# An FP4 fake-quantization moved wholly to VectorE, and its software pipelining taken out, in an attention + FFN block on eight cores

## The chip, the cores and the metric

The kernel runs on eight cores of one Trainium2 chip (two dies of four cores). Every core runs the same program on two of the sixteen sequences; nothing is exchanged between cores. The metric is the device time in microseconds of the slowest core. A core has TensorE (PE, matmuls and transposes), VectorE (DVE), ScalarE (ACT), GpSimd (POOL, here a little arithmetic in one stage and the issue of stores) and SyncE (SP, the issue of loads), each with its own in-order instruction stream. The streams meet only in semaphores.

## The reference

Input x is 16 x 2048 x 1024 in f32. Both branches start from the same LayerNorm, and their sum goes onto x:

```python
xn = _layernorm(x)
x = x + attn(xn, Wqkv, bqkv, Wproj, bproj, mapping) + ffn(xn, w_gate, w_up, w_down)

def fp4_quant_dequant(x):          # blocks of 16 along the last dim
    xb = x.reshape(shape[:-1] + (shape[-1] // 16, 16))
    scale = jnp.maximum(jnp.max(jnp.abs(xb), axis=-1, keepdims=True) / 6.0, 1e-12)
    xn = xb / scale
    idx = jnp.searchsorted(_MID, jnp.abs(xn))     # _MID  = .25 .75 1.25 1.75 2.5 3.5 5
    return (_GRID[idx] * jnp.sign(xn) * scale).reshape(shape)   # _GRID = 0 .5 1 1.5 2 3 4 6
def fp4_linear(x, w):
    return einsum('bsk,nk->bsn', fp4_quant_dequant(x), fp4_quant_dequant(w))
def ffn(x):
    h = silu(fp4_linear(x, w_gate)) * fp4_linear(x, w_up)      # 1024 -> 2816
    return fp4_linear(h, w_down)                               # 2816 -> 1024
```

The attention gathers queries and 64 keys per block of 64 rows by a Hilbert mapping, 16 heads of 64.

## The kernel before

A core has 4096 rows, 32 tiles of 128. After a short setup the stages follow each other with barriers between them:

- **Stage A** (once for each of the two sequences, 16 tiles each). A tile of x is loaded by SyncE. VectorE takes statistics (L448 to L455), ScalarE the square root (L484), VectorE applies them (L457, into `sc2`) and casts to bf16 (L462). The normalized tile is transposed on TensorE (L543) and multiplied with Wqkv in six chunks of 512 columns (L530, L533), each evacuated by ScalarE (L504) before POOL stores the tile to `qkv_dram`. The same tile is also quantized, transposed (L551), evacuated (L493, L517) and stored to `xqT_dram` for the FFN. Both transposes use the one PSUM tile `psT`.
- **Stages B and C** (once a sequence): gathers and attention, output projection, residual; the sum goes to `partial_dram`.
- **Weight stage**: 68 pieces of w_gate, w_up and w_down are quantized and transposed into SBUF. Here POOL adds up the three sign tiles.
- **Stage D** (32 tiles). SyncE loads the quantized transposed tile and the partial sum of tile gt. The load waits for the store of tile gt-2 (by the semaphore `sp`). TensorE computes three pairs of gate and up chunks (two chunks of 512, in the third pair 512 and 256; L1128), ScalarE takes Silu of the gate chunks (L1194, L1195) into `pairbuf`, and VectorE multiplies them with the up chunks (L1251, L1253) and quantizes the product into `hq2`. The quantized product of tile gt-1 is transposed in three groups (L1149), evacuated (L1208), multiplied with w_down (L1164), and added to the partial sum by VectorE (L1270, L1271), after which POOL stores it.

**Quantization.** Seven thresholds decide the level of a squared scaled value: four (`TL`) count 1 each, three (`TSQ`) count 1, 1 and 2 doubled. It is split in three helpers. `_q_pre` (VectorE, 5 instructions) takes the block maxima, scale and reciprocal, and the scaled value `v`. `_q_scal` (ScalarE, 4) squares `v` and takes Sign of the square against the three `TSQ` thresholds. A fifth ScalarE instruction takes the sign of `v`. `_q_post` (VectorE, 9 in stages A and D) adds up the `TL` compares in `sc5`, adds the three sign tiles, multiplies by the sign and by half the scale.

**Pipelining.** In A and D the quantization of a tile spreads over two rounds. VectorE's stream in round t is statistics, apply, `_q_pre` of tile t, then `_q_post` of tile t-1 (in D the same by pairs). ScalarE's stream in round t of stage A is: root of t; sign of t-1; evacuation of the quantized transpose of t-2; evacuation of the normalized transpose of t-1; six evacuations of QKV of t-1; `_q_scal` of t. TensorE's is: QKV of t-1; transpose of the normalized tile t; transpose of the quantized tile t, which waits for `_q_post` of t. In D ScalarE has for each pair: sign of the pair before; two Silus; `_q_scal` (its Sign tiles have one buffer and wait for the last `_q_post`); evacuation of one transpose group. TensorE has pairs 0 and 1 of gt, three transpose groups of gt-1, pair 2 of gt, the down product of gt-1. The values that semaphores have to reach are counted ahead in tables (`EVA`, `EVD`).

Of the kernel before, what the change touches and what calls it, by code (L numbers as in the profile page):

```python
# [8 lines left out]
F32 = mybir.dt.float32  # L9
BF16 = mybir.dt.bfloat16  # L10
# [12 lines left out]
NKC = D // 128  # L23
# [8 lines left out]
QPOST_S = 9  # L32
# [85 lines left out]
def build_nc(stage=9):  # L118
# [25 lines left out]
    with ExitStack() as st:  # L144
# [22 lines left out]
        uneg = sb("uneg", [128, 16], F32)  # L167

# [171 lines left out]
        with ExitStack() as g1:  # L340
# [40 lines left out]
            for seq in range(NSEQ if stage >= 5 else (1 if (stage >= 2 or stage >= 30) else 0)):  # L381
                if True:
# [4 lines left out]
                    vAb = [sc3, vA2]  # L387
                    a2Ab = [sc4, sc6]
# [3 lines left out]
                    svA, ssA, stnA, ldA, lgA, spA, sqA = sv.v, ss.v, stn.v, ld.v, lg.v, sp.v, sq.v  # L392

                    EVA = {}
                    cs, cv, cp, cq = ssA, svA, stnA, sqA
                    for t in range(T + 1):
                        if t <= T - 1:
                            cv += 5; EVA[("recip", t)] = cv
                            cv += 1; EVA[("apply", t)] = cv
                            cv += 1; EVA[("xnbf", t)] = cv  # L400
                            cv += QPRE_INCS; EVA[("v", t)] = cv
                        if t >= 1:
                            cv += QPOST_S
                            EVA[("post", t - 1)] = cv
                            EVA[("L3", t - 1)] = cv - 5
                            EVA[("srel", t - 1)] = cv - 2
                            EVA[("q1", t - 1)] = cv - 1
                        if t <= T - 1:
                            cs += 1; EVA[("rstd", t)] = cs
                        if t >= 1:  # L410
                            cs += 1; EVA[("sgn", t - 1)] = cs
                        if t >= 2:
                            cs += 1; EVA[("xqTev", t - 2)] = cs
                        if t >= 1:
                            cs += 1; EVA[("xnTev", t - 1)] = cs
                            for oc in range(6):
                                cs += 1; EVA[("qkvev", t - 1, oc)] = cs
                        if t <= T - 1:
                            cs += 1; EVA[("a2", t)] = cs
                            cs += 3; EVA[("s3", t)] = cs  # L420
                        if t == T:
                            cs += 1; EVA[("xqTev", T - 1)] = cs
                        if t >= 1:
                            for oc in range(6):
                                cp += 1; EVA[("qkvchunk", t - 1, oc)] = cp
                        if t <= T - 1:
                            cp += 1; EVA[("txn", t)] = cp
                            cp += 1; EVA[("txq", t)] = cp
                    ldav = lambda t: ldA + 16 * (t + 1)

                    with nc.Block() as blk:
                        @blk.sync
                        def _(sync):
                            for t in range(T):
                                if t >= 1:
                                    sync.wait_ge(ld.h, ldav(t - 1))
                                if t >= 2:
                                    sync.wait_ge(sv.h, EVA[("apply", t - 2)])
# [5 lines left out]
                        def _(vec):  # L444
                            for t in range(T + 1):
                                if t <= T - 1:
                                    vec.wait_ge(ld.h, ldav(t))
                                    sv.inc(vec.bn_stats(stats[:, 0:6], xbA[t % 2][:, 0:512]))  # L448
                                    sv.inc(vec.bn_stats(stats[:, 6:12], xbA[t % 2][:, 512:1024]))
                                    vec.wait_ge(sv.h, sv.v)  # L450
                                    sv.inc(vec.bn_aggr(stats[:, 12:14], stats[:, 0:12]))
                                    vec.wait_ge(sv.h, sv.v)
                                    sv.inc(vec.tensor_scalar_add(stats[:, 14:15], stats[:, 13:14], 1e-5))
                                    vec.wait_ge(sv.h, sv.v)
                                    sv.inc(vec.reciprocal(stats[:, 15:16], stats[:, 14:15]))  # L455
# [872 lines left out]
```

## Time and profile before

| | us |
|---|---|
| median of 3 runs | 6145.74 |
| lowest, highest | 6119.06, 6185.59 |
| the profiled execution | 6171.19 |
| span of its slowest core (core 7) | 6169.6 |
| span of its fastest core (core 0) | 6036.1 |

The profile is that of core 7. The busy time of an engine counts its instructions, not its waits. Lists of instructions in order of time give start, duration, engine, line, operation, output and inputs, and in brackets how long the engine stood idle before it and whose end released it. A time between two starts on one engine is a duration with its gap.

### The profile page before, as it was taken

Reading aid. Unit: us, or ns where it says so; the run is one execution under the profiler, and the core shown is the slowest. Engines: PE = TensorE matmul, PEld = TensorE weight load, DVE = VectorE, ACT = ScalarE, POOL = GpSimd, SP = SyncE. Lnnn points to the kernel's source line nnn. Section 1 sums busy time; section 2 is a strip of 40 time slices with the busy share of each in tenths; the row PEclk is TensorE's granted clock in tenths of the full one; section 3 lists DMA queues with packets and bytes.
Section 4 is the critical chain, followed back from the end, with each engine's and each line's share of the span. In section 5 each row is a group of like instructions: output and inputs, shape, how many; then the busy total and the mean of one; then the engine's idle time right before and its main releaser. Section 6 shows DMA issues by size and latency. Waiting matters only on the chain. (4 is left out here: it accounts for less than half of the span.)

```text
span 6169.6 us, 39885 instructions; the slowest of 8 cores (6036.1 to 6169.6 us)
## 1 busy us (share of the span) xinstructions
PE 2254.8 (37%) x12373; PEld 1094.2 (18%) x12373; DVE 3222.5 (52%) x3408; ACT 1567.2 (25%) x2218; POOL 713.2 (12%) x453
## 2 busy tenths in 40 slices
PE   1444447444444400000004444344344344344344
PEld 0111243111134100000001111112112112112111
DVE  2444332444423599999996544543544544544544
ACT  1222221222222133333432222221221221221221
POOL 0000011000011244444440000000000000000000
PEclk9666656666655755555556666666667667667666
DMA  4111113111111401101100000000000000000000
GB/s 75 37 41 39 43 47 111 55 40 41 39 51 42 133 27 31 31 28 29 32 25 13 15 17 17 9 17 17 9 17 17 9 17 17 9 17 17 9 17 16
DMA packets 86057, 196.70 MB, mean 32 GB/s; under 512 B 42295, under 2 KB 42311, under 8 KB 85847
## 3 DMA queue, kind: packets, MB, share of 16 engines
q1 hardware_dynamic: 59304, 93.42, 5.6%
q0 software_dynamic: 26544, 100.74, 5.2%
q8 instruction: 102, 1.67, 0.1%
q14 instruction: 107, 0.88, 0.0%
HBM read 135.41 MB, written 67.12 MB: 33 GB/s over the span
## 5 line engine op out<-in xcount | busy, mean ns | idle before, releaser
L98 DVE SCALAR_TENSOR_TENSOR sc<-sc 128x1024 f32<-128x1024 f32 (+1 forms) x588 | 691.8, 1176 | 62.7 <-DVE sc L98 1.4
L1251 DVE TENSOR_TENSOR sc<-pairbuf,psU 128x512 f32<-128x512 f32 x96 | 66.1, 688 | 1000.8 <-ACT pairbuf L1194 1000.8
L1164 PE MATMUL psA<-wdqT,hqT 128*128 128x512 bf16 x1408 | 386.4, 445 | 497.1 <-ACT hqT L1208 496.0
L969 PE MATMUL psT<-ident,wq_bf 128*128 128x128 bf16 x528 | 67.1, 306 | 1118.1 <-DVE wq_bf L115 1118.1
L1194 ACT ACTIVATE pairbuf<-psQ 128x512 f32<-128x512 f32 x96 | 56.8, 592 | 1213.6 <-PE psB L1128 1213.6
L1149 PE MATMUL psT<-ident,hq 128*128 128x128 bf16 x704 | 77.0, 273 | 781.6 <-ACT hqT L1208 771.4
L1279 POOL DMA_DIRECT2D out<-sc x32 | 17.1, 533 | 2897.2 <-DVE sc L1271 2805.4
L457 DVE TENSOR_SCALAR sc<-sc,stats 128x1024 f32<-128x1024 f32 x32 | 26.0, 813 | 562.4 <-ACT stats L484 562.4
L1164 PEld LDWEIGHTS psA<-wdqT,hqT 128*128 128x128 bf16 x1408 | 154.0, 111 | 722.7 <-issue 607.9
L969 PEld LDWEIGHTS psT<-ident,wq_bf 128*128 128x128 bf16 x528 | 50.9, 137 | 1134.3 <-issue 1134.3
L72 ACT ACTIVATE s1D<-sc,qbias 128x1024 bf16<-128x1024 f32 (+1 forms) x96 | 103.7, 1080 | 564.3 <-DVE sc L107 564.2
L530 PE MATMUL psQ<-Wqkv_sb,xnT 128*128 128x512 bf16 x768 | 239.2, 468 | 0.0
L504 ACT CAST qkv_tile<-psQ 128x512 bf16<-128x512 f32 x96 | 56.4, 587 | 674.0 <-PE psQ L533 674.0
L1270 DVE TENSOR_TENSOR sc<-psA,sc 128x512 f32<-128x512 f32 x32 | 22.1, 692 | 380.2 <-PE psA L1164 380.2
L1128 PE MATMUL psQ<-wgqT,attn_tm 128*128 128x512 bf16 x384 | 146.7, 551 | 198.7 <-DMA sc<-partial_dram 170.3
L80 POOL TENSOR_TENSOR sc<-s1W,s2W 128x1024 f32<-128x1024 bf16 (+1 forms) x68 | 147.2, 2164 | 620.3 <-DVE sc L98 451.5
L1128 PE MATMUL psQ<-wgqT,sexp 128*128 128x512 bf16 x384 | 145.0, 545 | 194.3 <-DMA sc<-partial_dram 174.9
L68 ACT ACTIVATE sc<-sc 128x1024 f32<-128x1024 f32 x132 | 134.7, 1020 | 293.7 <-DVE sc L63 293.6
L551 PE MATMUL psT<-ident,xq_tm 128*128 128x128 bf16 x256 | 32.4, 306 | 463.6 <-DVE xq_tm L115 463.6
L1149 PEld LDWEIGHTS psT<-ident,hq 128*128 128x128 bf16 x704 | 59.4, 122 | 801.3 <-issue 793.8
L530 PE MATMUL psU<-Wqkv_sb,xnT 128*128 128x512 bf16 x768 | 198.6, 405 | 0.0
L115 DVE TENSOR_TENSOR wq_bf<-sc,bstats 128x1024 bf16<-128x1024 f32 (+1 forms) x68 | 191.1, 2810 | 7.5 <-DVE sc L113 0.5
(192 smaller groups left out, 6258.4 us busy)
## 6 DMA issues: line engine op xcount, KB each, us to landing
sc<-xin SPq DMA_DIRECT2D x64, 512.0 KB
qkv_dram<-qkv_tile POOLq DMA_DIRECT2D x32, 768.0 KB, 4.5
partial_dram<-sc POOLq DMA_DIRECT2D x32, 512.0 KB, 3.8
sc<-partial_dram SPq DMA_DIRECT2D x32, 512.0 KB
out<-sc POOLq DMA_DIRECT2D x32, 512.0 KB, 3.0
wrow<-wg SPq DMA_DIRECT2D x22, 512.0 KB
wrow<-wu SPq DMA_DIRECT2D x22, 512.0 KB
xqT_dram<-xqTst POOLq DMA_DIRECT2D x32, 256.0 KB, 4.9
```

The costliest lines, as they stand in the source:

```text
L68: ss.inc(scal.activation(a2_ap, v_ap, AF.Square))
L72: ss.inc(scal.activation(s1_ap, a2_ap, AF.Sign, bias=qbias[:, 0:1]))
L80: sq.inc(g.tensor_tensor(u[:, 0:n], s1[:, 0:n], s2[:, 0:n], ALU.add))
L98: sv.inc(vec.scalar_tensor_tensor(L[:, 0:n], a2[:, 0:n], c, L[:, 0:n], ALU.is_gt, ALU.add))
L115: sv.inc(vec.tensor_tensor(seg(out_bf), seg(L[:, 0:n]), bc(hsc), ALU.mult))
L530: tensor.matmul(pq[:], xnTA[(t - 1) % 2][:, 128 * c:128 * (c + 1)], Wqkv_sb[:, c, 512 * oc:512 * (oc + 1)], start=(c == 0), stop=False)
L969: m = tensor.transpose(psT[:, 128 * k:128 * (k + 1)], wqW[c % 2][:, 128 * k:128 * (k + 1)], ident[:])
L1128: m = tensor.matmul(dst, xqb[gt % 2][:, 128 * c:128 * (c + 1)], w_src[:, c, i0:i0 + iw], start=(c == 0), stop=(c == NKC - 1))
L1149: m = tensor.transpose(psT[:, 128 * c:128 * (c + 1)], hq2[:, (gt - 1) % 2, 128 * (8 * g + c):128 * (8 * g + c + 1)], ident[:])
L1164: m = tensor.matmul(psA[:, 512 * oc:512 * (oc + 1)], hqT[:, 128 * c:128 * (c + 1)], wdqT[:, c, 512 * oc:512 * (oc + 1)], start=(c == 0), s ...
L1194: ss.inc(scal.activation(pb2[:, 0:iwA], gbank[0][:, 0:iwA], AF.Silu))
L1251: sv.inc(vec.tensor_mul(sc2[:, 0:iwA], pb2[:, 0:iwA], psU[:, 0:iwA]))
```

## The change

The pipelining of the quantization in stages A and D is taken out, and a single function of 19 VectorE instructions does all of it. Of these, `tensor_reduce` and three small ones prepare the scales, and 15 go over the whole tile.

```diff
+def _emit_quant(vec, x_ap, nblk, bstats, v, a2, L, S, out_bf, sv):
...
+    sv.inc(vec.tensor_reduce(sc, seg(x_ap), AX.X, ALU.max, apply_absolute_value=True))
+    vec.wait_ge(sv.h, sv.v)
+    sv.inc(vec.tensor_scalar(sc, sc, 1.0 / 6.0, 1e-12, ALU.mult, ALU.max))
+    vec.wait_ge(sv.h, sv.v)
+    sv.inc(vec.reciprocal(rsc, sc))
+    sv.inc(vec.tensor_scalar_mul(hsc, sc, 0.5))
+    vec.wait_ge(sv.h, sv.v)
+    sv.inc(vec.tensor_tensor(seg(v[:, 0:n]), seg(x_ap), bc(rsc), ALU.mult))
+    vec.wait_ge(sv.h, sv.v)
+    sv.inc(vec.tensor_mul(a2[:, 0:n], v[:, 0:n], v[:, 0:n]))
+    vec.wait_ge(sv.h, sv.v)
+    sv.inc(vec.tensor_single_scalar(L[:, 0:n], a2[:, 0:n], TL[0], ALU.is_gt))
+    for c in TL[1:]:
+        vec.wait_ge(sv.h, sv.v)
+        sv.inc(vec.scalar_tensor_tensor(L[:, 0:n], a2[:, 0:n], c, L[:, 0:n], ALU.is_gt, ALU.add))
+    sv.inc(vec.tensor_single_scalar(S[:, 0:n], a2[:, 0:n], TSQ[2], ALU.is_gt))
+    for c in (TSQ[1], TSQ[0], TSQ[2]):
+        vec.wait_ge(sv.h, sv.v)
+        sv.inc(vec.scalar_tensor_tensor(S[:, 0:n], a2[:, 0:n], c, S[:, 0:n], ALU.is_gt, ALU.add))
+    vec.wait_ge(sv.h, sv.v)
+    sv.inc(vec.scalar_tensor_tensor(L[:, 0:n], S[:, 0:n], 2.0, L[:, 0:n], ALU.mult, ALU.add))
+    sv.inc(vec.tensor_single_scalar(a2[:, 0:n], v[:, 0:n], 0.0, ALU.is_gt))
+    vec.wait_ge(sv.h, sv.v)
+    sv.inc(vec.tensor_scalar(a2[:, 0:n], a2[:, 0:n], 2.0, -1.0, ALU.mult, ALU.add))
+    vec.wait_ge(sv.h, sv.v)
+    sv.inc(vec.tensor_mul(L[:, 0:n], L[:, 0:n], a2[:, 0:n]))
+    vec.wait_ge(sv.h, sv.v)
+    sv.inc(vec.tensor_tensor(seg(out_bf), seg(L[:, 0:n]), bc(hsc), ALU.mult))
```

Stage A: VectorE quantizes tile t right after the cast of tile t, and there is no post in the next round. ScalarE loses the four activations of `_q_scal` and the sign; the evacuation of the quantized transpose of t-1 comes at the end of round t, after the six of QKV.

```diff
 @blk.scalar
 def _(scal):
     for t in range(T + 1):
         if t <= T - 1:
-            scal.wait_ge(sv.h, EVA[("recip", t)])
+            scal.wait_ge(sv.h, cva(t) + 5)
             ss.inc(scal.activation(stats[:, 14:15], stats[:, 15:16], AF.Sqrt))
         if t >= 1:
-            if t >= 2:
-                scal.wait_ge(sv.h, EVA[("q1", t - 2)])
-            ss.inc(scal.activation(sgnA[:], vAb[(t - 1) % 2][:], AF.Sign))
...
-        if t <= T - 1:
-            scal.wait_ge(sv.h, EVA[("v", t)])
...
-            _q_scal(scal, vAb[t % 2][:], a2Ab[t % 2][:],
...
+            scal.wait_ge(stn.h, txqv(t - 1))
+            ss.inc(scal.copy(xqTA[(t - 1) % 2][:], psT[:]))
```

Stage D: VectorE quantizes each pair's product in one go. ScalarE loses its five activations a pair and takes two copies more: it brings the up chunks from PSUM into a `pairbuf` twice as wide, and VectorE's product reads both factors from there. TensorE has the pairs 0, 1, 2 of gt, then the transposes and the down product of gt-1. ScalarE evacuates the three transpose groups after the three pairs.

```diff
+                ss.inc(scal.activation(pb2[:, 0:iwA], gbA[:, 0:iwA], AF.Silu))
+                ss.inc(scal.activation(pb2[:, 512:512 + iwB], gbB[:, 0:iwB], AF.Silu))
+                ss.inc(scal.copy(pb2[:, 1024:1024 + iwA], psU[:, 0:iwA]))
+                ss.inc(scal.copy(pb2[:, 1536:1536 + iwB], psB[:, 512:512 + iwB]))
...
-                sv.inc(vec.tensor_mul(sc2[:, 0:iwA], pb2[:, 0:iwA], psU[:, 0:iwA]))
+                vec.wait_ge(ss.h, spair(gt, pq, 2))
+                sv.inc(vec.tensor_mul(sc2[:, 0:iwA], pb2[:, 0:iwA], pb2[:, 1024:1024 + iwA]))
+                vec.wait_ge(ss.h, spair(gt, pq, 3))
...
+                _emit_quant(vec, sc2[:, 0:pw], pw // 16, bstats,
+                            sc3, sc4, sc5, sc6,
+                            hq2[:, gt % 2, pair_cols[pq][0]:pair_cols[pq][0] + pw], sv)
```

In both stages a load still waits for what it waited for, in D for the store of tile gt-2. In the weight stage only the offsets inside `bstats` change (72 to 88, 144 to 176, 288 to 352). The second buffers of `v` and the sign tiles of A and D are gone, and `maskU` is allocated earlier.

## Rows read from the trace of the kernel before

**Rows 1.** The page's busy times: us, share of the span, instructions.

```profile
PE 2254.8 (37%) x12373; PEld 1094.2 (18%) x12373; DVE 3222.5 (52%) x3408; ACT 1567.2 (25%) x2218; POOL 713.2 (12%) x453
```

**Rows 2.** Stretches: length, busy us (count) by engine, granted clock, DMA share, GB/s.

```profile
98.75:705.72 606.97, 263.46 (x1058) 103.83 (x1058) 271.58 (x336) 167.49 (x218) 21.66 (x30) 0.68 0.12 39
1102.25:1703.15 600.90, 256.85 (x1058) 102.89 (x1058) 271.58 (x336) 167.50 (x218) 21.67 (x30) 0.66 0.12 40
3257.56:6162.56 2905.00, 1231.62 (x5190) 552.05 (x5190) 1381.69 (x1600) 645.47 (x775) 16.54 (x31) 0.69 0.05 15
```

**Rows 3.** In order of time, stage A, VectorE: start, us, line, idle before.

```profile
475.02 1.23 DVE L115 TENSOR_TENSOR xq_tm<-sc,bstats 128x1024 bf16<-128x1024 f32 x1
476.16 0.69 DVE L448 BATCH_NORM_STATS2 stats<-sc 128x6 f32<-128x512 f32 x1
...
497.94 0.81 DVE L457 TENSOR_SCALAR sc<-sc,stats 128x1024 f32<-128x1024 f32 x1 [19.65 <-ACT stats L484]
...
499.65 1.22 DVE L56 TENSOR_REDUCE bstats<-sc 128x64 f32<-128x1024 f32 x1
```

**Rows 4.** The same stretch, TensorE and ScalarE.

```profile
462.45 1.01 ACT L497 COPY xnT<-psT 128x1024 bf16<-128x1024 bf16 x1 [1.25 <-PE psT L543]
...
476.54 1.01 PE L551 MATMUL psT<-ident,xq_tm 128*128 128x128 bf16 x8 [14.17 <-DVE xq_tm L115]
...
477.34 3.38 PE L530 MATMUL psQ<-Wqkv_sb,xnT 128*128 128x512 bf16 x8
...
480.97 1.90 PE L530 MATMUL psU<-Wqkv_sb,xnT 128*128 128x512 bf16 x8
...
492.82 0.59 ACT L504 CAST qkv_tile<-psU 128x512 bf16<-128x512 f32 x1 [1.98 <-PE psU L533]
...
497.64 0.19 ACT L484 ACTIVATE stats<-stats 128x1 f32<-128x1 f32 x1
```

**Rows 5.** The instructions of line L1270: min/median/max ns, first and last start.

```profile
L1270 DVE TENSOR_TENSOR sc<-psA,sc x32: 691/692/693, 3389.4 to 6161.3; 128x512 f32<-128x512 f32 x32
```

**Rows 6.** Who waited for whom: us in total, times, longest.

```profile
DVE sc L1251 <- ACT pairbuf L1194: 1000.8, 96, 20.8
```

**Rows 7.** In order of time, stage D, VectorE and TensorE.

```profile
3513.96 0.69 DVE L1251 TENSOR_TENSOR sc<-pairbuf,psU 128x512 f32<-128x512 f32 x1 [2.51 <-ACT pairbuf L1194]
...
3515.34 1.22 DVE L56 TENSOR_REDUCE bstats<-sc 128x64 f32<-128x1024 f32 x1
...
3517.68 1.23 DVE L63 TENSOR_TENSOR sc<-sc,bstats 128x1024 f32<-128x1024 f32 x1
3519.01 0.69 DVE L95 TENSOR_SCALAR sc<-sc 128x1024 f32<-128x1024 f32 x1
...
3519.81 3.88 DVE L98 SCALAR_TENSOR_TENSOR sc<-sc 128x1024 f32<-128x1024 f32 x3
...
3539.48 0.69 DVE L1251 TENSOR_TENSOR sc<-pairbuf,psU 128x512 f32<-128x512 f32 x1 [9.08 <-ACT pairbuf L1194]
...
3540.61 0.95 DVE L56 TENSOR_REDUCE bstats<-sc 128x48 f32<-128x768 f32 x1
...
3542.55 0.96 DVE L63 TENSOR_TENSOR vD<-sc,bstats 128x768 f32<-128x768 f32 x1
...
3576.29 3.53 PE L1128 MATMUL psQ<-wgqT,sexp 128*128 128x512 bf16 x8 [9.80 <-DMA sc<-partial_dram]
...
3585.85 0.69 DVE L1251 TENSOR_TENSOR sc<-pairbuf,psU 128x512 f32<-128x512 f32 x1 [17.90 <-ACT pairbuf L1194]
...
6136.60 0.69 DVE L1270 TENSOR_TENSOR sc<-psA,sc 128x512 f32<-128x512 f32 x1 [11.93 <-PE psA L1164]
```

**Rows 8.** VectorE by line and form, busy us, mean ns: weight stage, setup.

```profile
L101 DVE SCALAR_TENSOR_TENSOR sc<-sc 128x1024 f32<-128x1024 f32 x60 | 180.3, 3006 | 6.2
...
L262 DVE TENSOR_SCALAR map_rowf<-map_rowf 1x2048 f32<-1x2048 f32 x1 | 1.2, 1214 | 0.1
```

**Rows 9.** The page's DMA issues: count, KB each, us to landing.

```profile
xqT_dram<-xqTst POOLq DMA_DIRECT2D x32, 256.0 KB, 4.9
```

More of the change, by code:

```diff
@@ new lines, in build_nc, with cva, csa, cpa @@
+                    svA, ssA, stnA, ldA, lgA, spA = sv.v, ss.v, stn.v, ld.v, lg.v, sp.v
+                    def cva(t):
+                        return svA + 26 * t
+                    def csa(t):
+                        return ssA + (9 * t - 8 if t >= 1 else 0)
+                    def cpa(t):
+                        return stnA + (8 * t - 6 if t >= 1 else 0)
+                    def sc_off(t):
+                        return 1 if t <= T - 1 else 0
+                    rstdv = lambda t: csa(t) + 1
@@ L429, in build_nc @@
+                    xnTev = lambda tm1: csa(tm1 + 1) + sc_off(tm1 + 1) + 1
+                    qkvev = lambda tm1, oc: csa(tm1 + 1) + sc_off(tm1 + 1) + 2 + oc
+                    xqTev = lambda tm1: csa(tm1 + 1) + sc_off(tm1 + 1) + 8
+                    qkvchunk = lambda tm1, oc: cpa(tm1 + 1) + oc + 1
+                    txnv = lambda t: cpa(t) + (6 if t >= 1 else 0) + 1
+                    txqv = lambda t: txnv(t) + 1
                     ldav = lambda t: ldA + 16 * (t + 1)
@@ new lines, in build_nc, with cpf, csf, cvf @@
+            svD, ssD, stnD, ldD, soutD, spD = sv.v, ss.v, stn.v, ld.v, sout.v, sp.v
+            def cpf(gt):
+                v = stnD
+                for g in range(gt):
+                    v += (3 if g <= NTOT - 1 else 0) + (4 if g >= 1 else 0)
+                return v
+            def csf(gt):
+                v = ssD
+                for g in range(gt):
+                    v += (12 if g <= NTOT - 1 else 0) + (3 if g >= 1 else 0)
+                return v
+            def cvf(gt):
+                v = svD
+                for g in range(gt):
+                    v += (63 if g <= NTOT - 1 else 0) + (2 if g >= 1 else 0)
+                return v
@@ new lines, in pairv, with tgroup, down_done, spair @@
+            def pairv(gt, pq):
+                return cpf(gt) + pq + 1
+            def tgroup(gtm1, g):
+                gt = gtm1 + 1
+                return cpf(gt) + (3 if gt <= NTOT - 1 else 0) + g + 1
+            def down_done(gtm1):
+                return tgroup(gtm1, 2) + 1
+            def spair(gt, pq, k):
+                return csf(gt) + 4 * pq + k + 1
+            def evacv(gtm1, g):
+                gt = gtm1 + 1
+                return csf(gt) + (12 if gt <= NTOT - 1 else 0) + g + 1
@@ L1083, in ldv, with hmultv, quantdonev, addsv @@
+            def hmultv(gt, ci):
+                pq, k = ci // 2, ci % 2
+                return cvf(gt) + 21 * pq + k + 1
+            def quantdonev(gt):
+                return cvf(gt) + 63
+            def addsv(gtm1):
+                return cvf(gtm1 + 1) + 63 * (1 if gtm1 + 1 <= NTOT - 1 else 0) + 2
             def ldv(gt):
@@ L1204, in _ @@
[L1204 to L1217 removed]
+                                    gbA = gbank[0]
```

430 lines of the change are left out of this document (113 added, 317 removed).

## The prediction

> **What bounds the kernel now.** I read the page's busy times first [rows 1]: VectorE leads with 3222.5 us of 6169.6, only 52%, so no engine is full, and the question is in which stage VectorE is full and in which it waits. The stretches by stage [rows 2] answer that. The two passes of stage A (LayerNorm, quantize, QKV) take 607.0 and 600.9 us with VectorE busy 271.6 in each, 45%; stage D (the FFN) takes 2905.0 us with VectorE busy 1381.7, 48%. TensorE is at 43% in all three. So in A and D the time is set by a loop of waits. The rest (setup, attention, projection, weight quantization; 2057 us by difference) is the same in both kernels but for offsets of buffers. I take it as unchanged.
>
> Stage A's VectorE rows show the loop [rows 3]: a tile takes 607.0 / 16 = 37.9 us there, of which 19.65 are one wait for ScalarE's square root L484 (at 497.94). ScalarE's and TensorE's rows [rows 4] show why: the root of tile t+1 stands behind the four activations of `_q_scal`, these behind the six evacuations of QKV of tile t-1, and these behind the matmuls, which need `_q_post` of t-1 for the transpose ahead of them. VectorE does that post in the same round. Everything is in one ring.
>
> Stage D's adds stand at 3389.4 (first) and 6161.3 (last) [rows 5]. The last tile has no tile behind it, and its adds come 24.7 us after those before (6136.60 [rows 7]), so a tile takes (6161.3 - 24.7 - 3389.4) / 30 = 91.6 us. VectorE's waits inside it: L1251 1000.8 us in 96 waits [rows 6], 31.3 a tile. 2.5 of them come ahead of the second pair, 9.1 ahead of the third, and about 19.7 ahead of the first. The last is seen in [rows 7]: after the adds store and load run, TensorE starts 3576.29, L1251 3585.85, 17.90 us after the adds' end; the longest is 20.8 [rows 6].
>
> **The change, part by part.** It does three things: (a) quantization goes wholly to VectorE (`_emit_quant`, 19 instructions for 14, the compares against `TSQ`, the square and the sign among them); (b) each tile is quantized in one go, not half in the next round, so ScalarE has only the root and evacuations in A, and Silu and evacuations in D; (c) in D ScalarE also copies the up product out of PSUM, and TensorE's third pair moves ahead of the transposes.
>
> Cost of one quantization of 1024 columns, start to start, from [rows 7]. Reduce to scaled value is 3515.34 to 3517.68, 2.34, with the three small ones inside. A two-input operation behind a wait takes 1.33 (3517.68 to 3519.01), a one-input compare 0.80 (3519.01 to 3519.81). The new function has 11 of the first kind (scaled value, square, 3+3 compare-adds, combine, sign multiply, output) and 4 of the second. Two kinds are new. A compare without a second constant is in setup, 2048 f32 elements in 1.21 us (L262 [rows 8]), 0.59 ns each, the rate of the 0.69 row, so it keeps that price. A tile multiplied by itself has no row: 1.23 as any two-input operation, or, as it reads one tile, 0.69 at the least; I take 1.23, for it is still a two-input instruction, and keep 0.54 x 128 = 68 us for the range's low side. Three instructions wait for nothing just before them (the first `S` compare, the sign compare, the next tile's first); such a one starts about 0.09 before the former's end instead of 0.10 after (475.02 + 1.23 against 476.16 [rows 3]), 0.19 less each. 2.34 + 11 x 1.33 + 4 x 0.80 - 0.57 = 19.6 us. For 768 columns: 1.94 (3540.61 to 3542.55) + 11 x 1.06 + 4 x 0.66 (estimated from 0.80 by the ratio of the long ones) - 0.57 = 15.7.
>
> Stage A, VectorE alone: statistics 497.94 - 19.65 - 476.16 = 2.13, the root's round trip 0.4 (0.30 from L484's start to L457's [rows 3, 4], and a hop before), apply and cast 1.71 (497.94 to 499.65), quantization 19.6: 23.8 us a tile. Is anything slower? The root of t+1 starts a second chain: evacuation of xnT 1.01, transpose and QKV up to the last evacuation 476.54 to 492.82, 16.3, its 0.6, the evacuation of xqT (of the size of xnT's) 1.0, hops 0.2, about 19.1, after which ScalarE is free for root t+2. That is 4.7 under 23.8. SyncE's load waits for the apply of t-2, a round early. POOL's two stores stand behind the xqT evacuation at 19.1, take 1.4 to issue (21.66 / 30 each [rows 2]) and 4.9 to land [rows 9]: 1.6 into the next round, where the first QKV evacuation, which waits for them, is due at 1.2 + 4.4 (476.54 to 480.97, where the second chunk follows [rows 4]) = 5.6. So 4.0 spare. A pass is 16 x 23.84 and about 1 for its start, an estimate, 382.5, against 607.0 and 600.9: minus 224.5 and minus 218.4, together 443. Ends are alike: after the last quantization transpose, QKV and stores follow in both.
>
> Stage D, VectorE alone: from the product to the reduce 1.38 (1024) and 1.13 (768) [rows 7], so 2 x 21.0 + 16.8 + adds 1.3 = 60.1 us. The two waits inside a tile (2.5, 9.1) and the one before the adds go: TensorE has 38.5 us of work a tile (1231.6 / 32 [rows 2]), with this tile's pairs first and then the transposes and the down product of the one before, while VectorE quantizes for 59. The wait ahead of the first pair stays, because the load of gt+1 waits for the store of gt-1, that for the adds of gt-1, and VectorE does these after quantizing gt. It grows: the product now waits for Silu A, Silu B and the copy of the up half instead of Silu A. ScalarE starts 0.49 apart and a copy of this size out of PSUM is about 0.59, so 0.97 (bounds: 0.5, one start apart, and 1.2, two whole ones). 20.0 (between 19.7 and 20.8) + 1.0 + 60.1 = 81.1 against 91.6, 30 times: minus 315. The ends I take as cancelling: the first two tiles, which wait for no store, lose a few us by the longer quantization, and the last, whose product needs no post after the adds before it, gains as many.
>
> Sum: 6169.6 - 443 - 315 = 5412 us of span. The profiled execution ran 1.6 over its span, 6171.2, and that is 25.5 over the median of the runs, 6145.7. That gives 5388, and I say 5390, for the median.
>
> What is hidden costs if its cover goes: were it the TensorE chain in A that ends last, each us beyond 4.7 costs 32; each us that the first pair is late costs 30.
>
> **Rivals.**
> TensorE slows. Its first eight matmuls behind a gap take 3.38 at 1.2 GHz, the later eights 1.9 at 2.4 GHz [rows 4]; the granted clock of both stages is 0.66 to 0.69 [rows 2]. In D its gap before the first pair grows from 9.8 [rows 7] to some 35 us. Against: it falls back after the present gaps already, and comes up within the first eight or ten. If it never came up, A's chain would be 19.1 + 5 x 1.7 = 27.6, 3.8 over, times 32 = 120; D's first pair 3 x 1.7 = 5 later, times 30 = 150: 5660.
>
> POOL and VectorE hinder each other. In the weight stage, where POOL computes, one combine takes 3.01 us [rows 8] against 1.23. In A POOL issues 1.4 us of stores a tile into a VectorE that now has no gap. If VectorE stood still for them: 46 us; if they landed twice as late (9.8), 0.9 beyond the spare, 29 us more: 5465. Against: the stores already issue beside VectorE's work at unchanged durations. The Trainium skill, SBUF — State Buffer, section "SBUF: two separate sides", says that a DMA issued by GpSimd cannot write its descriptors while VectorE runs an operation in a two-port mode, and gives 620 ns that became some 3100. The kernel adds three such one-input operations to each quantization. By that page's figures a store would be 2.5 us late, an estimate, and be inside the spare. No row here shows such a wait; the 4.9 us are what the stores take now.
>
> The other side: the tiles stay chained. Should the root still come only after the newest QKV, A keeps its 19.65 us: 23.4 + 19.7 = 43.1 against 37.8, plus 5.3 x 32 = 170; should D keep its 2.5 and 9.1, it is 92.7 against 91.6, plus 33: 6350. VectorE's added work then shows bare (4.5 us per 1024, some 550 in all). It decides from 758 us of waits that stay, 11.8 a tile over the 64 of both stages. For it speaks only that the ring exists now; against it, that no instruction on ScalarE ahead of the root needs VectorE's output of the same round any more.
>
> **How the numbers follow.** My forecast 80%, TensorE slow 7%, POOL 7%, chained 4%, something unseen 2%. The forecast's own range: the wait before the first pair 17.9 to 20.8 (minus 63, plus 24), the copy (minus 15, plus 6), a gap of 0.10 off by 0.02 in 16 places of 128 quantizations (41 either way); not all at their ends at once, 5300 to 5440. The square at 0.69 (minus 68) would reach the low end with any other of these. The POOL case and the first part of the TensorE case are taken in: 5300 to 5520. About 1% is what a measurement of this kernel tells from no change. Faster 0.95, same 0.01, slower 0.04.
>
> **What would show it.** In the new trace: no wait of VectorE for the root beyond 0.4; an A pass of 383 us with VectorE at 97%; quantizations of 19.6 us; in D one wait of 19 to 22 us a tile and nearly none else, period 81; VectorE busy near 3770, ScalarE far below its 1567 (five activations a quantization go, two copies a pair come in D), POOL unchanged. I am wrong if A's round is set by the evacuation of xqT, if QKV's evacuation waits for stores, or if the first pair of a tile takes over 11 us.

## The result and the profile after

| | us |
|---|---|
| after, median of 10 runs | 5374.68 (5364.07 to 5386.49) |
| before, median of 10 runs | 6117.34 (6068.37 to 6185.59) |
| ratio, 95% interval | 0.8797 [0.8769, 0.8825] |
| profiled execution after: span of its slowest core (core 3) | 5362.1 |

The forecast was 5390, 15 us above. The profiled spans differ by 6169.6 - 5362.1 = 807.5 us, where the working had 758. The 6169.6 belongs to one of the longer executions of before, in which cores 4 to 7 ran for a median of 6155.7 and cores 0 to 3 for 6042.4 with the same program (after: 5354.2 and 5355.0).

The page's busy times, after (columns as in [rows 1]):

```profile
PE 2114.4 (39%) x12373; PEld 1039.0 (19%) x12373; DVE 3737.3 (70%) x4048; ACT 1030.1 (19%) x1770; POOL 716.4 (13%) x453
```

The stretches of the first pass of stage A and of stage D, after (columns as in [rows 2]):

```profile
96.95:480.36 383.41, 244.94 (x1058) 96.71 (x1058) 341.20 (x416) 85.50 (x138) 21.68 (x30) 0.81 0.19 61
2835.00:5355.00 2520.00, 1119.80 (x5147) 506.40 (x5145) 1760.37 (x2079) 268.82 (x476) 16.55 (x31) 0.72 0.05 16
```

VectorE has 515 us more to do than in [rows 1], and the kernel is 743 us faster in the medians. Both stages have given up waits. VectorE's waits after (us in total, times, longest), where [rows 6] had 1000.8 in 96:

```profile
DVE sc L1154 <- ACT pairbuf L1133: 598.3, 31, 21.0
DVE sc L1166 <- PE psA L1109: 17.2, 1, 17.2
DVE sc L471 <- ACT stats L488: 15.8, 32, 1.7
```

Before's waits for the root were 562.4 us in 32 (one of them the 19.65 us of [rows 3]); they have shrunk to 15.8. In stage D one wait a tile is left.

**Stage A.** A pass is 383.4 us (first statistics 96.95, those of the second pass 480.36), against the 607.0 and 600.9 of [rows 2]. ScalarE in one tile, in order of time, beside VectorE's first statistics and its apply:

```profile
312.91 0.69 DVE L462 BATCH_NORM_STATS2 stats<-sc 128x6 f32<-128x512 f32 x1
315.12 0.20 ACT L488 ACTIVATE stats<-stats 128x1 f32<-128x1 f32 x1 [5.26 <-DVE stats L469]
315.43 0.81 DVE L471 TENSOR_SCALAR sc<-sc,stats 128x1024 f32<-128x1024 f32 x1 [0.40 <-ACT stats L488]
...
332.17 0.59 ACT L497 CAST qkv_tile<-psU 128x512 bf16<-128x512 f32 x1 [1.27 <-PE psU L516]
332.65 1.02 ACT L500 COPY xqTst<-psT 128x1024 bf16<-128x1024 bf16 x1
339.28 0.20 ACT L488 ACTIVATE stats<-stats 128x1 f32<-128x1 f32 x1 [5.61 <-DVE stats L469]
```

A VectorE tile is 336.71 - 312.91 = 23.80 us. The chain of the other engines, from the root to the end of the evacuation of the quantized transpose, is 315.12 to 333.67 = 18.55 us, and after it ScalarE stands idle for 5.61 us until the next root can start. In [rows 3] and [rows 4] it was VectorE that stood and the root that was late.

**Stage D.** One handover between tiles, all engines in order of time (SPq is SyncE's queue):

```profile
4141.64 0.68 DVE L1167 TENSOR_TENSOR sc<-psA,sc 128x512 f32<-128x512 f32 x1
4142.88 0.53 POOL L1174 DMA_DIRECT2D out<-sc  x1 [79.96 <-DVE sc L1167]
4146.00 0.37 SPq L1054 DMA_DIRECT2D attn_tm<-xqT_dram  x1
4150.48 3.57 PE L1083 MATMUL psQ<-wgqT,attn_tm 128*128 128x512 bf16 x8 [38.93 <-DMA sc<-partial_dram]
4159.65 0.60 ACT L1131 ACTIVATE pairbuf<-psQ 128x512 f32<-128x512 f32 x1 [59.30 <-PE psB L1083]
4160.62 0.59 ACT L1133 COPY pairbuf<-psU 128x512 f32<-128x512 f32 x1
4161.31 0.69 DVE L1154 TENSOR_TENSOR sc<-pairbuf 128x512 f32<-128x512 f32 x1 [19.00 <-ACT pairbuf L1133]
4180.44 1.86 PE L1109 MATMUL psA<-wdqT,hqT 128*128 128x512 bf16 x4 [1.23 <-ACT hqT L1139]
```

The 19.00 us of VectorE's idle time have parts that can be read here: 3.7 us from the end of the adds until SyncE issues the load, for which the store has to be issued and to land (4142.3 to 4146.0), 4.5 until TensorE, waiting for that load, starts (4150.48), 9.2 for the first pair (4159.65), 1.7 for the two Silus and the copy. The down product begins at 4180.44 and ends about 12 us later; the next adds come at 4220.09. So the wait inside a tile and the wait ahead of the adds [rows 7] are gone. The adds of the tiles run from 2951.6 to 5335.44 (the last but one): 30 periods of 79.5 us, where it was 91.6.

### The profile page after: what moved, and what is told of

Same layout as the page of the kernel before. It is cut to its first block and busy times, and to the rows that moved or that the text cites. A ratio compares the mean times of both kernels' runs of the same rounds, so it can differ in the third digit from the quotient of the medians.

```text
span 5362.1 us, 39202 instructions; the slowest of 8 cores (5347.6 to 5362.1 us)
## 1 busy us (share of the span) xinstructions
PE 2114.4 (39%) x12373; PEld 1039.0 (19%) x12373; DVE 3737.3 (70%) x4048; ACT 1030.1 (19%) x1770; POOL 716.4 (13%) x453
## 5 line engine op out<-in xcount | busy, mean ns | idle before, releaser
L1154 DVE TENSOR_TENSOR sc<-pairbuf 128x512 f32<-128x512 f32 x96 | 66.0, 688 | 598.3 <-ACT pairbuf L1133 598.3
L73 DVE SCALAR_TENSOR_TENSOR sc<-sc 128x1024 f32<-128x1024 f32 (+1 forms) x384 | 444.8, 1158 | 41.1 <-DVE sc L70 0.9
L69 DVE SCALAR_TENSOR_TENSOR sc<-sc 128x1024 f32<-128x1024 f32 (+1 forms) x384 | 444.8, 1158 | 41.1 <-DVE sc L69 1.4
L1131 ACT ACTIVATE pairbuf<-psQ 128x512 f32<-128x512 f32 x96 | 57.3, 597 | 2139.1 <-PE psB L1083 1927.3
L1083 PE MATMUL psQ<-wgqT,sexp 128*128 128x512 bf16 x384 | 117.1, 460 | 609.6 <-DMA sc<-partial_dram 579.8
L1083 PE MATMUL psQ<-wgqT,attn_tm 128*128 128x512 bf16 x384 | 116.5, 458 | 609.2 <-DMA sc<-partial_dram 566.5
L135 DVE SCALAR_TENSOR_TENSOR sc<-sc 128x1024 f32<-128x1024 f32 (+1 forms) x204 | 247.0, 1211 | 22.3 <-DVE sc L135 0.9
L150 DVE TENSOR_TENSOR sc<-sc,sgnW 128x1024 f32<-128x1024 f32 (+1 forms) x68 | 184.3, 2711 | 14.4 <-DVE sc L138 10.9
L121 POOL TENSOR_TENSOR sc<-sc,s3W 128x1024 f32<-128x1024 f32 (+1 forms) x68 | 191.8, 2821 | 9.7
L119 POOL TENSOR_TENSOR sc<-sc,s3W 128x1024 f32<-128x1024 f32 (+1 forms) x68 | 190.2, 2798 | 11.2 <-POOL sc L117 2.2
L513 PE MATMUL psU<-Wqkv_sb,xnT 128*128 128x512 bf16 x768 | 187.1, 387 | 0.0
L138 DVE SCALAR_TENSOR_TENSOR sc<-sc 128x1024 f32<-128x1024 f32 (+1 forms) x68 | 182.0, 2676 | 7.1
L725 DVE TENSOR_TENSOR sc<-psA,maskU 128x1024 f32<-128x1024 f32 x16 | 19.6, 1225 | 238.0 <-PE psA L662 238.0
L1083 PEld LDWEIGHTS psQ<-wgqT,sexp 128*128 128x128 bf16 x384 | 39.3, 111 | 681.7 <-issue 659.4
```

The costliest lines, as they stand in the source:

```text
L69: sv.inc(vec.scalar_tensor_tensor(L[:, 0:n], a2[:, 0:n], c, L[:, 0:n], ALU.is_gt, ALU.add))
L73: sv.inc(vec.scalar_tensor_tensor(S[:, 0:n], a2[:, 0:n], c, S[:, 0:n], ALU.is_gt, ALU.add))
L119: sq.inc(g.tensor_tensor(u[:, 0:n], u[:, 0:n], s3[:, 0:n], ALU.add))
L121: sq.inc(g.tensor_tensor(u[:, 0:n], u[:, 0:n], s3[:, 0:n], ALU.add))
L135: sv.inc(vec.scalar_tensor_tensor(L[:, 0:n], a2[:, 0:n], c, L[:, 0:n], ALU.is_gt, ALU.add))
L138: sv.inc(vec.scalar_tensor_tensor(L[:, 0:n], u[:, 0:n], 0.0, L[:, 0:n], ALU.add, ALU.add))
```

## The experiments

All are compared with the kernel before on the same chip: its median was 6065.5 us beside e1 to e4, 6068.1 beside e0 and e5 to e7, and 6125.5 beside e8 and e9, which ran on another chip. There the seven runs of before lie between 6065 and 6177, so the ratios of e8 and e9 are less sharp than the others (see their intervals), and these two are best compared with each other. Differences in us are differences of medians.

### The two stages by themselves

e1 takes the change in stage A alone, e2 in stage D alone. Below, `-` is the call in before; the one stage takes the `+`, the other keeps the `-`.

```diff
-    _q_pre(vec, sc2[:], 64, bstats, 72 * (t % 2), vAb[t % 2], sv)        # e1: stage A
-    _q_scal(scal, vAb[t % 2][:], a2Ab[t % 2][:], ...)
-    _q_post(vec, 64, bstats, 72 * (b % 2), a2Ab[b % 2], ...)
+    _emit_quant(vec, sc2[:], 64, bstats, sc3, sc4, sc5, sc6, ...)
...
-    _q_scal(scal, vDb[Pg % 2][:, 0:pw], a2Db[Pg % 2][:, 0:pw], ...)      # e2: stage D
+    ss.inc(scal.copy(pb2[:, 1024:1024 + iwA], psU[:, 0:iwA]))
+    ss.inc(scal.copy(pb2[:, 1536:1536 + iwB], psB[:, 512:512 + iwB]))
+    _emit_quant(vec, sc2[:, 0:pw], pw // 16, bstats, sc3, sc4, sc5, sc6, ...)
```

> Only stage A is changed (quantization in one go on VectorE); stage D is as before. Theory (the change breaks a ring of waits in A and another in D, and the two gains add): a pass of A takes 383 us, D keeps its 88.5 to 92 us a tile; 5700 us, 414 less than the 6117 of before, the rest of the 742 being D's. Rival (the gain in D alone matters, or the two stages hinder each other): less than 300 us gained.

> Only stage D is changed; stage A is as before. Theory: passes of A stay at 590 to 607 us, D falls to 79.5 us a tile; 5790 us, some 328 less than before, so that this gain and that of the run with A alone add up to the 742 of the whole change within 20. Rival (they overlap): the two together are over 30 off.

> The changed kernel unedited, to stand beside its variants on one chip. 5375 us; on a chip where the kernel before takes 6065 the gain is 690 and equals the sum of the runs with A alone (421) and D alone (262) within 20.

Measured: e1 5650.69 us, ratio 0.9306 [0.9291, 0.9322]; e2 5800.46, 0.9568 [0.9552, 0.9584]; e0 5377.58, 0.8856 [0.8832, 0.888].

In medians e1 is 415 us under its before, e2 265, and the whole change 690.5. The parts add up to 680 (683, if each is worked out from its ratio), which the intervals can't tell from 690: no meddling of the two stages is seen. Stage A came out as priced (415 for 414). Stage D came out 63 us short of the 328 expected. The reason is in the profile of before itself. The price rests on its core 7. These are VectorE's waits on core 0 in the same execution:

```profile
DVE sc L1251 <- ACT pairbuf L1194: 920.3, 96, 18.3
DVE sc L457 <- ACT stats L484: 531.6, 32, 19.0
```

Core 7 has 1000.8 [rows 6] where core 0 has 920.3, 2.5 us a tile more, and its longest wait is 20.8 against 18.3. A tile of before takes 91.6 us on core 7 and 88.7 on core 0 (first adds 3341.4, last but one 6003.4), so what is worth 91.6 - 79.5 = 12.1 us a tile on core 7 is worth 9.2 on core 0: 30 x 9.2 = 276, near the 265. In e1, whose stage D is that of before, core 6 also has tiles of 88.8 us.

The wait ahead of a tile's first product is where core 7 differs: 20.6 us in all but the first five of its thirty handovers, 17.7 to 18.3 on core 0. In the mean of thirty, TensorE starts 6.0 us after the issue of the load on core 7 and 4.6 on core 0, and the first pair takes 9.6 and 8.85 us. Why, stays open.

### Was it VectorE's new work, or the order?

e3 leaves everything of before as it is but TensorE's order in stage A: QKV of tile t follows its own transpose, ahead of the quantized transpose of t. ScalarE keeps square and signs.

```diff
 @blk.tensor
 def _(tensor):
-    for t in range(T + 1):
-        if t >= 1:
-            tensor.wait_ge(ss.h, EVA[("xnTev", t - 1)])
-            for oc in range(6):                    # QKV of t-1
...
+    for t in range(T):
         ...                                        # transpose of the normalized tile t
+        tensor.wait_ge(ss.h, EVA[("xnTev", t)])
+        for oc in range(6):                        # QKV of t
...
         tensor.wait_ge(sv.h, EVA[("post", t)])     # transpose of the quantized tile t
```

> The kernel before with one edit: in stage A TensorE's QKV matmuls of a tile come ahead of the transpose of its quantized form, not behind it. ScalarE keeps its square and signs, VectorE its 11 long operations, and the quantization stays spread over two rounds. Theory (the ring of before ran through that order; where the arithmetic is done does not matter for it): the wait for the root falls from 17 us to about 5, a tile of A from 37 to 24 to 25.5 us, 5700 us. Rival (the gain in A needs the four activations to leave ScalarE, ahead of the root): at least 12 us of the wait stay, over 6000 us.

Measured: 5626.78 us, ratio 0.9283 [0.9268, 0.9299], minus 439. The stretch of a pass of stage A in e3 (columns as above):

```profile
97.10:478.50 381.40, 249.46 (x1072) 97.12 (x1073) 268.88 (x334) 167.77 (x219) 21.65 (x30) 0.80 0.20 62
```

VectorE's wait for the root in e3 (in total, times, longest):

```profile
DVE sc L456 <- ACT stats L483: 147.1, 32, 5.5
```

One root in e3 with what stands ahead of it on ScalarE and waits for it on VectorE, in order of time:

```profile
324.72 1.13 ACT L76 ACTIVATE s3A<-sc,qbias 128x1024 bf16<-128x1024 f32 x1
325.76 0.19 ACT L483 ACTIVATE stats<-stats 128x1 f32<-128x1 f32 x1
326.06 0.81 DVE L456 TENSOR_SCALAR sc<-sc,stats 128x1024 f32<-128x1024 f32 x1 [5.08 <-ACT stats L483]
```

Without moving one instruction to VectorE, stage A is as fast as in the changed kernel: a pass takes 381.4 us where that of after takes 383.4. VectorE is busy for 268.9 us of it and not for 341, and 4.6 us a tile are still spent waiting for a root that stands behind the last Sign (324.72) on ScalarE. So what stage A gained, it gained from the ring being cut. The 4.5 us of work a tile that went to VectorE took up what was left of the wait, and no more. (The same has not been tried in stage D: no run changes TensorE's order there and leaves the quantization as it was.)

### The wait that is left in stage D

e4 is the changed kernel with the two loads of a tile parted. The activations of tile gt+1 are loaded as soon as their buffer is free, and only the partial sum still waits for the store of tile gt-1. e7 does the same to the kernel before.

```diff
+def load_x(gt):
+    if gt >= 1:
+        sync.wait_ge(ld.h, ldv(gt - 1))
+    if gt >= 2:
+        sync.wait_ge(stn.h, pairv(gt - 2, 2))
+    sync.dma_start(out=xqb[gt % 2], in_=xqT_dram[...]).then_inc(ld.h, 16)
+load_x(0)
 for gt in range(NTOT):
-    if gt >= 2:
-        sync.wait_ge(sp.h, spD + gt - 1)
-        sync.wait_ge(stn.h, pairv(gt - 2, 2))
-    sync.dma_start(out=xqb[gt % 2], in_=xqT_dram[...]).then_inc(ld.h, 16)
-    sync.dma_start(out=pp[gt % 2], in_=partial_dram[...]).then_inc(ld.h, 16)
+    if gt + 1 < NTOT:
+        load_x(gt + 1)
+    if gt >= 1:
+        sync.wait_ge(lp.h, lgv(gt - 1))
+    if gt >= 2:
+        sync.wait_ge(sp.h, spD + gt - 1)
+    sync.dma_start(out=pp[gt % 2], in_=partial_dram[...]).then_inc(lp.h, 16)
```

> The changed kernel, in D with the load of the quantized tile apart from that of the partial sum: TensorE's input of tile gt+1 is loaded a tile earlier and no longer waits for the store of gt-1. Theory (the 19.2 us ahead of a tile's first product are the store, the load and the first pair in a row): all of it is hidden, a tile of D takes 60.1 us, 30 x 19.2 = 576 less: 4800 us, VectorE busy over 95% in D. Rival (another wait takes its place: TensorE has 38 us of work a tile and its first pair comes only behind the down product): 8 to 10 of the 19 stay, 5050 to 5100 us.

> The kernel before with the load of D's quantized tile apart from that of the partial sum, as in the variant of the changed kernel. Theory (in the kernel before the 18 us ahead of the first pair are store, load and first pair behind the down product; the split takes out store and load, 8.4, and TensorE's order keeps the pair of about 9 behind the down product): the wait falls from 18 to 9, minus 270, 5800 us. Rival (the store is the whole wait): minus 530. Rival (the other waits grow as much): no change.

Measured: e4 4777.0 us, ratio 0.7883 [0.7868, 0.7899], 600.6 us under e0 on the same chip. e7 5717.39, ratio 0.9409 [0.9362, 0.9457], minus 351. The handover in e4:

```profile
3549.86 0.68 DVE L1182 TENSOR_TENSOR sc<-psA,sc 128x512 f32<-128x512 f32 x1
3550.46 0.68 DVE L1169 TENSOR_TENSOR sc<-pairbuf 128x512 f32<-128x512 f32 x1
3551.11 0.53 POOL L1189 DMA_DIRECT2D out<-sc  x1 [59.45 <-DVE sc L1182]
3554.20 0.33 SPq L1072 DMA_DIRECT2D sc<-partial_dram  x1
3554.68 0.36 SPq L1059 DMA_DIRECT2D sexp<-xqT_dram  x1
```

The first product (L1169) follows the adds without a gap: its pair was done before the store was even issued. The whole 19 us were the road from the adds through store, load and pair: the adds now come every 60.1 us, as expected, where they came every 79.5. ("VectorE busy over 95% in D" was missed in the same way as the 97% of the prediction: it is 1648.08 of 1803.00 us, 91%, since the gaps between its instructions don't count.) The same handover in e7, where before's order is kept:

```profile
4059.67 5.34 PE L1179 MATMUL psA<-wdqT,hqT 128*128 128x512 bf16 x24
4064.85 1.89 PE L1143 MATMUL psQ<-wgqT,attn_tm 128*128 128x512 bf16 x8
4065.19 0.69 DVE L1285 TENSOR_TENSOR sc<-psA,sc 128x512 f32<-128x512 f32 x1 [11.99 <-PE psA L1179]
4072.77 0.69 DVE L1266 TENSOR_TENSOR sc<-pairbuf,psU 128x512 f32<-128x512 f32 x1 [6.29 <-ACT pairbuf L1209]
```

Here the load is off the path too, but TensorE has the down product of gt-1 ahead of the first pair of gt, and the adds wait for the one and the product for the other. The wait fell from 17.90 [rows 7] to 6.29, 11.6 us; times 30 that is 348, near the 351 measured, and between the 270 and the 530 of the two expectations. The theory let 9 us stay, the whole first pair behind a gap. (On core 2 of e7 all but one of the thirty waits are 6.29.) Two things make it 6.3: the first eight matmuls take 1.89 right behind the down product, where they took 3.53 behind a gap of 9.80 [rows 7], and the pair begins 0.3 us ahead of the adds (4064.85, 4065.19) and so runs beside them. What e4 has over e7 in stage D goes with the order of the changed kernel, in which the down product runs while VectorE is busy with the next tile. That it is the order alone is argued from these rows and not shown: the two kernels also differ in where the quantization is done.

### Whose time is the changed kernel's?

e5 takes the second count out of the new function, five of its 19 instructions (so its quantization knows fewer levels). e6 lets the product read the up half from PSUM, without ScalarE's two copies.

```diff
-    sv.inc(vec.tensor_single_scalar(S[:, 0:n], a2[:, 0:n], TSQ[2], ALU.is_gt))                # e5
-    for c in (TSQ[1], TSQ[0], TSQ[2]):
...
-        sv.inc(vec.scalar_tensor_tensor(S[:, 0:n], a2[:, 0:n], c, S[:, 0:n], ALU.is_gt, ALU.add))
...
-    sv.inc(vec.scalar_tensor_tensor(L[:, 0:n], S[:, 0:n], 2.0, L[:, 0:n], ALU.mult, ALU.add))
...
-    ss.inc(scal.copy(pb2[:, 1024:1024 + iwA], psU[:, 0:iwA]))                                 # e6
-    ss.inc(scal.copy(pb2[:, 1536:1536 + iwB], psB[:, 512:512 + iwB]))
...
-    sv.inc(vec.tensor_mul(sc2[:, 0:iwA], pb2[:, 0:iwA], pb2[:, 1024:1024 + iwA]))
+    sv.inc(vec.tensor_mul(sc2[:, 0:iwA], pb2[:, 0:iwA], psU[:, 0:iwA]))
```

> The changed kernel without the second count: the first S compare, its three compare-adds and the combine are left out of each quantization (the levels above 2 come out wrong), 14 instructions a quantization instead of 19, 5.9 us less on 1024 columns and 4.7 on 768. Theory (VectorE sets the end everywhere in A and D, with TensorE's and ScalarE's chain about 19 us a tile behind it in A): D falls by its full 2 x 5.9 + 4.7 = 16.5 us a tile, A only from 23.8 to 19, not to 17.9: minus 530 and minus 150, 4690 us. Rival (A has no second chain so near): 17.9 us a tile, 4655 us. Rival (VectorE is not what sets the end in D): D falls by less than half.

> The changed kernel, in D with VectorE's product reading the up chunks from PSUM as before; ScalarE's two copies a pair go, and TensorE's next up chunks wait for the product. Theory: the wait ahead of a tile's first product falls by the two instructions between Silu A and copy A, 0.97 us, and TensorE's later up chunks stay hidden: 30 x 0.97 = 29 less than the changed kernel, 5345 us. Rival (TensorE's third pair, now held until the second product 21 us later, pushes transposes and down product past the adds): slower than the changed kernel.

Measured: e5 4715.9 us, ratio 0.7774 [0.776, 0.7788], 662 under e0. e6 5335.05, 0.8795 [0.8779, 0.881], 42.5 under e0. VectorE's waits in e5, for the pair and for the root:

```profile
DVE sc L1149 <- ACT pairbuf L1128: 609.3, 31, 21.5
DVE sc L466 <- ACT stats L483: 43.3, 32, 2.5
```

And in e6, for the pair:

```profile
DVE sc L1155 <- ACT pairbuf L1133: 578.7, 31, 20.5
```

e5: a quantization of 1024 columns is 5.72 us shorter there and one of 768 is 4.53. In stage D all of it comes off the end, since the wait stays where it was, at 19.6 us ((609.3 - 21.5) / 30; 19.2 in after, 20.1 in e0): 2 x 5.72 + 4.53 = 15.97, times 31 that is 495. In stage A the wait for the root grows from 0.5 to 1.35, because the other engines' chain of 18.55 us is now longer than VectorE's work in a tile (23.80 - 5.72 = 18.1): (5.72 - 0.86) x 32 = 156. Together 651 of the 662. So in the changed kernel VectorE's own work stands bare in both stages, and in stage A about 5 us deep.

e6: its wait is 18.6 us a tile ((578.7 - 20.5) / 30), that of after 19.2 ((598.3 - 21.0) / 30), and that of e0, the same kernel on e6's chip, 20.1. That makes 19 to 45 us, around the 29 expected for one copy a tile. Like cores tell it finer. A tile of D takes 79.65 us in after and 78.87 in e6 on core 0, and 79.46 and 78.55 on core 3: 23 and 27 us over the stage. The rest of the 42.5 is not shown to come from the copies. On their way to the first adds of stage D, through work that is the same in both kernels, cores of one execution of after already spread by 19 us (core 0 at 2932.7, core 3 at 2951.6).

### Two kernels beyond the change

e5 said that each VectorE instruction counts, e4 that nothing else is late. e8 is e4 with the same quantization in 16 instructions. e9 is e4 with e6's product from PSUM.

```diff
-    sv.inc(vec.tensor_scalar_mul(hsc, sc, 0.5))
-    sv.inc(vec.tensor_single_scalar(S[:, 0:n], a2[:, 0:n], TSQ[2], ALU.is_gt))
-    for c in (TSQ[1], TSQ[0], TSQ[2]):
+    sv.inc(vec.tensor_scalar(S[:, 0:n], a2[:, 0:n], TSQ[2], 2.0, ALU.is_gt, ALU.mult))
+    for c in (TSQ[1], TSQ[0]):
...
-    sv.inc(vec.tensor_single_scalar(a2[:, 0:n], v[:, 0:n], 0.0, ALU.is_gt))
-    sv.inc(vec.tensor_scalar(a2[:, 0:n], a2[:, 0:n], 2.0, -1.0, ALU.mult, ALU.add))
+    sv.inc(vec.tensor_scalar(a2[:, 0:n], v[:, 0:n], 0.0, -0.5, ALU.is_gt, ALU.add))
...
-    sv.inc(vec.tensor_tensor(seg(out_bf), seg(L[:, 0:n]), bc(hsc), ALU.mult))
+    sv.inc(vec.tensor_tensor(seg(out_bf), seg(L[:, 0:n]), bc(sc), ALU.mult))
```

> The changed kernel with the split load of e4_split_load and a shorter form of the same quantization on VectorE: the count that enters twice is made by one comparison times 2 instead of two comparisons, the sign by one comparison minus 0.5 instead of two instructions (with the scale itself in the last product instead of its half), so that 16 instructions stand for 19. Theory: once the load is split VectorE sets the pace in both stages, so each removed slot comes off the end: in 1024 columns 1.33 + 0.80 + 0.05 = 2.18 us, in 768 columns 1.06 + 0.66 + 0.05 = 1.77 us; stage A 32 x 2.18 = 70 us, stage D 32 x (2 x 2.18 + 1.77) = 196 us, together 266 us off the 4777 of e4_split_load: 4510, with a tile of stage D at 54.0 us and one of stage A at 21.7. Rival: the chain of a tile through the other engines is long enough by now (18.6 us in stage A, and the three pairs, the transposes and the down product in stage D) that waits come back in stage A or D; if half of the gain goes so, 4640.

> The changed kernel with the split load of e4_split_load and the products of stage D read from PSUM as in e6_from_psum, without ScalarE's copies. Theory: the 42 us that e6_from_psum gave were a shorter road from TensorE to the first product of a tile while VectorE stood waiting there; with the load split nothing waits there, so nothing is left to gain: 4777 as e4_split_load, within 15. Rival: the copies cost VectorE or TensorE time by themselves (PSUM banks that come free later), then it gives about 40 us again: 4735. A second rival: a product that reads PSUM is slower than one that reads SBUF, by up to 0.1 us for each of the 192, and the time is up to 20 us longer.

Measured: e8 4515.0 us, ratio 0.7404 [0.7348, 0.7461]. e9 4782.69, 0.7836 [0.778, 0.7893]. For e8, the wait for the root in stage A and the adds at a handover of stage D with what follows them:

```profile
317.41 0.81 DVE L468 TENSOR_SCALAR sc<-sc,stats 128x1024 f32<-128x1024 f32 x1 [0.40 <-ACT stats L485]
...
3025.23 0.68 DVE L1177 TENSOR_TENSOR sc<-psA,sc 128x512 f32<-128x512 f32 x1
3026.43 0.68 DVE L1165 TENSOR_TENSOR sc<-pairbuf 128x512 f32<-128x512 f32 x1
```

e8 is 5 us off the 4510 that slots alone gave, with no wait come back. Its adds go from 2863.3 to 4482.8 in 30 periods of 54.0 us, as expected. It is the fastest of all, 26% under before. On its own chip e8 is 268 us under e9, where 266 were worked out. And e9 is 4783 against e4's 4777 on the other chip, with ratios whose intervals overlap, and with tiles of D of 60.1 us in both: with the load parted, the copies cost nothing that is seen, nor does reading from PSUM. The same copies were on the path in the changed kernel, and hidden as soon as the wait around them was.

## Why the prediction was right

**The price of one quantization.** 19.6 us for 1024 columns. After: the reduce at 317.14, the next tile's statistics at 336.71, 19.57. The two new kinds of instruction, and one without a wait behind one that has been waited for:

```profile
320.80 1.23 DVE L64 TENSOR_TENSOR sc<-sc 128x1024 f32<-128x1024 f32 x1
322.13 0.69 DVE L66 TENSOR_SCALAR sc<-sc 128x1024 f32<-128x1024 f32 x1
322.93 3.88 DVE L69 SCALAR_TENSOR_TENSOR sc<-sc 128x1024 f32<-128x1024 f32 x3
326.73 0.69 DVE L70 TENSOR_SCALAR sc<-sc 128x1024 f32<-128x1024 f32 x1
```

The product of a tile with itself takes 1.23 us like one of two tiles (the low side of the range had it at 0.69), the compare without a second constant takes 0.69, and L70, which waits for nothing just before it, starts 0.08 before the end of the one ahead. For 768 columns 15.7 was worked out and 15.73 is in the trace of e4.

**Stage A.** 23.84 us a tile were worked out and 23.80 measured, a pass 382.5 and 383.4. The second chain was given 19.1 and took 18.55. The root's wait is 0.40 in most tiles and 1.7 at most. So minus 443 became 607.0 + 600.9 - 2 x 383.4 = minus 441.

**Stage D.** VectorE's part was right: 60.1 and 79.5 - 19.2 = 60.3. The copy term was right, 0.97, as the starts of L1131 and L1133 (4159.65, 4160.62) show. The term that was missized is the wait itself: 20.0 was put in for it, between 19.7 and 20.8, though the one handover shown had 17.90 [rows 7]. That handover was one of the first five of core 7, and the later ones took 20.6, so 20.0 was right for that core; on core 0 all thirty were at 17.7 to 18.3, and the cores of after ran like core 0. With 17.9 the period would have been 79.0, and 79.5 is what came (the 0.4 left is TensorE's, see below). From 81.1 to 79.5 is 1.6 us a tile, 48 us, and nearly the whole gap between the 807 us that the spans show and the 758 of the sum.

That only 15 us are left of it in the medians is luck. The forecast took 24 us off the span to come to a median (5412 to 5388), because the profiled execution of before lay above the median of its runs. The one of after lies below its own: the median is 12.6 above the span. These two hide 36 of the 49 us.

**One sign that I had put wrong.** "VectorE at 97%" in an A pass: it shows 341.20 of 383.41, 89%. The sum of start-to-start slots would have been full; the view counts the instructions without the 0.10 us between them. Less far off were "busy near 3770", which is 3737.3, and the wait "of 19 to 22 us" in D, which is 18.4 to 20.6.

**The rivals.** TensorE hardly slowed: its gap before the first pair is now 38.93 us, the first eight matmuls take 3.57 and the third eight 1.89. The second eight take 1.89 in some handovers of after and up to 3.1 in others, so that the first pair, from its first matmul to its Silu, takes 9.2 us in the mean of thirty, where it took 8.85 on core 0 of before: 0.4 us a tile, 11 in all, of the 150 that the rival had. In stage A TensorE is granted 0.81 where it had 0.68. POOL and VectorE did not hinder each other. Two stores amid VectorE's work in after:

```profile
166.78 0.69 DVE L78 TENSOR_SCALAR sc<-sc 128x1024 f32<-128x1024 f32 x1
167.11 0.55 POOL L541 DMA_DIRECT2D qkv_dram<-qkv_tile  x1 [22.34 <-ACT xqTst L500]
167.65 0.91 POOL L543 DMA_DIRECT2D xqT_dram<-xqTst  x1
```

The stores are issued in the middle of VectorE's work, and both keep their durations: POOL's issues sum to 21.68 us in the pass, [rows 2] has 21.66. When they land, the trace of after does not give; that of e4, with the same stage A, does (count, KB each, median us from issue to landing):

```profile
qkv_dram<-qkv_tile POOLq DMA_DIRECT2D x32, 768.0 KB, 3.8
xqT_dram<-xqTst POOLq DMA_DIRECT2D x32, 256.0 KB, 4.4
```

So the stores do not land later than in before, where the second took 4.9 [rows 9]. The rule of the Trainium skill that stood beside this rival (SBUF — State Buffer, "SBUF: two separate sides": VectorE's two-port mode holds up the descriptors of a GpSimd DMA) is not seen at work. In six of the fifteen tiles of the pass the QKV store is issued while the one-input operation L78 still runs, as above, for 0.36 us at most, and takes no longer; a longer overlap, which would be a harder test, this pass does not show. That no QKV evacuation was held up is seen in the tile of 23.80. The tiles did not stay chained, in neither stage.

What the prediction did not see, since the sum did not need it: stage A would have gained as much by the order alone (e3). It read the ring rightly, but gave the move of work to VectorE and the cut of the ring as one thing.

## What to carry to other kernels

Where two engines wait for each other in a ring, look for the instruction that is queued behind work it does not need, and move that first: e3 got the whole gain of stage A by one change of order, and e4 got 600 us by giving two loads a semaphore each, so that the one TensorE needs no longer waits for a store. Only when no wait is left does an engine's work count one for one, and then instructions are worth removing (e8), while those that lie under another engine's work are worth nothing (e9). And read a wait's length on more than one core: the one taken from core 7 was 2 us a tile too long for the other cores.

## What was unexpected of the hardware

- TensorE's granted clock rises as its work moves closer together, though nothing was done to the matmuls: 0.68 in before's stage A pass and 0.81 after; in stage D 0.69 before [rows 2], 0.72 after, 0.77 in e4 and 0.80 in e8. The busy time of the same 1058 matmuls of a pass fell from 263.5 to 244.9 us. In these runs the kernels with fewer holes got some TensorE time back.

  Thirty tiles of stage D in e4, and below thirty in e8 (length, busy us and count of PE, PEld, DVE, ACT, POOL, granted clock, DMA share, GB/s):

```profile
2948.00:4751.00 1803.00, 1059.43 (x4764) 491.60 (x4764) 1648.08 (x1950) 249.76 (x442) 16.01 (x30) 0.77 0.07 22
```

```profile
2864.00:4484.00 1620.00, 1040.13 (x4683) 490.43 (x4768) 1484.55 (x1682) 249.68 (x442) 16.01 (x30) 0.80 0.08 25
```

- An instruction of VectorE behind its own semaphore starts 0.10 us after the end of the one ahead, and one without starts 0.08 before it. A quantization of 1024 columns lasts 19.57 us from start to start, and its 19 instructions sum to 18.4: 1.2 us are these gaps.
